# A decoder layer on one core: prologue, buffers and orders rebuilt

## The reference

```
q, k, v = x @ Wq + bq, x @ Wk + bk, x @ Wv + bv        # 16 heads of 8
q, k = rope(q), rope(k)                                # interleaved rotation
x = layernorm(x + softmax(q k^T / sqrt(8)) v)
x = layernorm(x + dense(cross_attention(x, ctx, mask)))  # ctx: 64 rows a batch, 16 heads
x = layernorm(x + relu(x @ W1 + b1) @ W2 + b2)         # 128 -> 512 -> 128
```

## Time and profile before

| what | us |
|---|---|
| median of three runs | 266.21 (264.18 to 266.30) |
| the profiled execution | 263.25 |
| its span, first to last instruction | 261.4 |
| mean granted TensorE clock, share of full | 0.944 |

### The profile page before, as it was taken

One profiled execution on the slowest core, in us unless ns is written; L12 is line 12 of the kernel. 1 busy time (PEld: TensorE's weight loads), 2 busy tenths in 40 slices (PEclk: granted clock), 3 DMA queues, 4 the chain that ended last, 5 costly groups with the idle time before them and its releaser, 6 DMA issues.

```text
span 261.4 us, 5399 instructions
## 1 busy us (share of the span) xinstructions
PE 220.7 (84%) x1734; PEld 169.8 (65%) x1734; DVE 189.4 (72%) x434; ACT 158.3 (61%) x296; POOL 82.9 (32%) x89
## 2 busy tenths in 40 slices
PE   0715757979998999999989999999999998988871
PEld 0503434847766768767757877967887776966661
DVE  5524845998995989979879977779557758474562
ACT  0089051847749666878914897648898455647330
POOL 9933026285543526013410121121011414113231
PEclk9985555999999999999999999999999999999998
DMA  5089991258476235143263034400031042300001
GB/s 191 0 240 292 338 225 38 73 160 265 127 216 192 94 110 168 49 144 119 73 188 115 4 93 159 128 3 16 5 93 61 3 140 78 80 4 21 20 20 43
DMA packets 21531, 28.67 MB, mean 110 GB/s; under 512 B 5248, under 2 KB 16768, under 8 KB 21376
## 3 DMA queue, kind: packets, MB, share of 16 engines
q1 hardware_dynamic: 21160, 27.87, 35.5%
q10 hardware_dynamic: 344, 0.46, 0.6%
HBM read 15.21 MB, written 11.27 MB: 101 GB/s over the span
## 4 chain that ended last, share of the span: by engine, by line
PE 50%; issue 14%; DVE 10%; DMA 9%; POOL 4%; ACT 2%; SPq 1%; DVEq 0%; POOLq 0%; ACTq 0%
PE bank L561 8%; PE scores L524 8%; PE scores L544 7%; PE bank L713 4%; DMA z_self<-qk_parts 4%; PE bank L702 3%; PE scores L619 3%; DMA q_rows<-z_self 3%; DVE neg_max L1413 2%; PE scores L622 2%; PE bank L656 2%; POOL rstd L1873 2%; PE scores L642 2%; PE scores L643 2%; DMA z_qx<-qx_parts 2%
## 5 line engine op out<-in xcount | busy, mean ns | idle before, releaser
L1413 DVE TENSOR_REDUCE neg_max<-scores 128x4 f32<-128x1024 f32 x64 | 76.3, 1219 | 15.6 <-PE scores L524 15.5
L1111 ACT ACTIVATE probs<-scores 128x1024 f32<-128x1024 f32 x64 | 64.0, 1026 | 7.5 <-PE scores L544 6.7
L524 PE MATMUL scores<-k_diag,q_rows 96*128 96x512 f32 x128 | 45.7, 463 | 11.4 <-DMA k_diag<-z_self 6.7
L544 PE MATMUL scores<-q_rows,k_diag 128*128 128x256 f32 x256 | 43.3, 300 | 1.3 <-ACT probs L1111 0.8
L544 PEld LDWEIGHTS scores<-q_rows,k_diag 128*128 128x128 f32 x256 | 35.6, 194 | 9.3 <-issue 7.6
L1873 POOL TENSOR_TENSOR rstd<-var_eps,minus_half 128x2 f32<-128x2 f32 x24 | 16.7, 698 | 66.6 <-DVE var_eps L1446 66.5
L524 PEld LDWEIGHTS scores<-k_diag,q_rows 96*128 96x128 f32 x128 | 22.9, 210 | 20.1 <-issue 18.0
L561 PE MATMUL bank<-probs,v_ones 128*32 128x256 f32 x512 | 30.9, 382 | 0.2
L1102 ACT CAST q_rows<-bank 8x128 fp32r<-8x128 f32 x64 | 16.3, 255 | 20.4 <-PE bank L532 19.3
L1413 DVE TENSOR_REDUCE neg_maxx<-scores 128x16 f32<-128x1024 f32 x16 | 19.4, 1223 | 8.7 <-PE scores L622 8.6
L561 PEld LDWEIGHTS bank<-probs,v_ones 128*32 128x32 f32 x512 | 16.3, 109 | 10.9 <-issue 3.4
(11 more groups left out here) (107 smaller groups left out, 385.1 us busy)
## 6 DMA issues: line engine op xcount, KB each, us to landing
z_self<-qk_parts SPq DMA_DIRECT2D x23, 256.0 KB, 3.2
q_rows<-z_self SPq DMA_DIRECT2D x8, 384.0 KB, 3.5
qx_slots<-z_qx SPq DMA_DIRECT2D x8, 384.0 KB, 3.4
k_diag<-z_self SPq DMA_DIRECT2D x30, 96.0 KB
z_qx<-qx_parts SPq DMA_DIRECT2D x8, 256.0 KB, 2.3
qk_swapped<-qk SPq DMA_DIRECT2D x14, 128.0 KB, 2.5
later_sb<-later SPq DMA_DIRECT2D x1, 1347.0 KB, 9.1
z_qx<-qx_parts SPq DMA_DIRECT2D x8, 128.0 KB, 2.5
```

Source lines behind the costliest of these rows:

```text
L524: mm = pe.matmul(score(use, b)[:, h * S:(h + 2) * S], qr_r[0:NROWS, b % 2, g, t * P:(t + 1) * P], kd_r[0:NROWS, b % 2, h:h + 2, g, :], sta ...
L544: mm = pe.matmul(score(use, b)[:, (2 * j + kt) * S:(2 * j + kt + 1) * S], kd_r[:, b % 2, 2 * half + j, g, kt * P:(kt + 1) * P], qr_r[:, b ...
L1111: ins = nc.scalar.activation(probs[:, g, 2 * half:2 * half + 2, :, :], score(use, b), ACT.Exp)
L1413: ins = nc.vector.tensor_reduce(out, score(use, b).rearrange("p (h k) -> p h k", k=SC if g == "x" else S), AX.X, ALU.max, negate=True)
```

## The change

- **Packs.** Instead of first, second and later there are six: wq and wk with their swapped columns, the tables at half the width (cos and sin once, not for q and k apart), wv with the identity, the cross-attention's constants, the FFN's. The factor 1/sqrt(8) leaves the tables and becomes the scale of the exp.
- **Queues.** ScalarE's queue loads the wv pack and xT of batch 0, the sync queue the rest. xT of batches 2 to 7 is issued before batch 0's images. The cross constants, context and FFN constants go later, one by one. x is loaded into xT's tile, so it waits for all projections.
- **Two batches rotated by VectorE.** Batches 0 and 1 both have swapped projections. VectorE does products, sums and low parts, q and k apart; ScalarE makes the high parts.
- **Projections.** q, k and v of the other batches stand between the first projections and batch 0's and 1's scores. They are copied to tiles of their own (qk for six batches, v_rows for eight). POOL instead of VectorE places v.
- **Warm-up.** Five matmuls on zeros stand first in TensorE's list. ScalarE's small exp moves near the end of its list.
- **Head rows.** ScalarE writes those of one buffer of k and of the cross k; a DMA copies them to the other.
- **Buffers.** x1_bias has eight, z_qx eight. Small PSUM uses may stand in any of the five spaces. The tables of uses and the step lists of all engines are new: cross-attention and FFN of early batches stand later in them than before.
- **Output.** It is stored in the order of partitions and reordered on the host; x is read in such an order too.

```diff
-FIRST = [("ident", P), ("wq", D), ("wk", D), ("bq", 1), ("bk", 1), ("wqs", D), ("wks", D), ("bqs", 1), ("bks", 1), ("head_of_row", HQ)]
-SECOND = [("cos", 2 * S), ("sin", 2 * S), ("wv", D), ("bv", D)]
+WQ = [("wq", D), ("wqs", D), ("bq", 1), ("bqs", 1)]
+WK = [("wk", D), ("wks", D), ("bk", 1), ("bks", 1)]
+ROPE = [("cos", S), ("sin", S)]
+WV = [("wv", D), ("bv", D), ("ident", P), ("head_of_row", HQ)]
+CROSS = [("wqx", D), ("wkx", D), ("wvx", D), ("bqx", 1), ("bkx", 1), ("bvx", D), ("mask", S), ("key_of_row", SC)]
+FFN = [("dense", D), ("w1", FF), ("w2", FC * D), ("b1", FC), ("dense_b", D), ("b2", D)]
...
         def misc(use, b):
-            return bank[:, SPACES.index(TURN[use, b][0]) - 3, :]
+            at = SPACES.index(TURN[use, b][0])
+            return scores[:, at, 0:512] if at < 3 else bank[:, at - 3, :]
...
+            def load_x():
+                for b in range(B):
+                    for use in ("qp", "kp", "v") if b < 2 else ("qkp", "v"):
+                        sp.wait_ge(*made(use, b))
+                sp.dma_start(x_res, x_d).then_inc(xres_in, 16)
...
+            load_xT(1)
+            load_wk()
+            load_rope()
+            load_wq()
+            load_other_xT()
+            first_image_high(0, 0)
+            first_image_low(0, 0)
+            first_image_low(0, 1)
+            load_q(0)
+            load_first_k()
+            first_image_high(1, 0)
+            first_image_high(1, 1)
+            first_image_low(1, 1)
+            first_image_low(1, 0)
+            swap(2)
+            load_q(1)
+            load_cross()
+            other_diag_heads()
+            load_ctxT()
+            load_k(1)
+            swap(3)
+            load_x()
+            images_low(2)
+            images_high(2)
+            load_ffn()
+            swap(4)
+            load_q(2)
+            load_k(2)
...
+            def warm_up():
+                pe.wait_ge(y_zeroed, 1)
+                for _ in range(5):
+                    pe.matmul(bank[:, 1, 0:S], y[:, 0, :], y[:].rearrange("p t d -> p (t d)"), start=True, stop=True)
+
+            def first_proj(b, j):
...
+                pe.matmul(o[:, 0:S], const(w), xT[:, b, :], start=True, stop=True)
+                mm = pe.matmul(o[:, S:2 * S], const(w + "s"), xT[:, b, :], start=True, stop=True)
...
+            warm_up()
+            first_proj(0, 1)
+            first_proj(0, 0)
+            first_proj(1, 1)
+            v_proj(1)
+            first_proj(1, 0)
+            qk_proj(2)
+            qk_proj(7)
+            v_proj(7)
+            qk_proj(5)
+            v_proj(5)
+            v_proj(2)
+            qk_proj(3)
+            v_proj(6)
             max_scores(0, 0, 0)
             max_scores(0, 0, 1)
+            v_proj(4)
+            max_scores(0, 1, 1)
+            max_scores(0, 1, 0)
+            qk_proj(4)
...
+            def first_high(b, j):
+                act.wait_ge(first_sum[j], b + 1)
...
+                nc.scalar.copy(qk_parts[:, 2 * j, :].bitcast(F32R), qk_rope[:, j, :]).then_inc(first_hi[j], 1)
...
+            def v_copy(b):
+                act.wait_ge(*made("v", b))
+                ins = nc.scalar.copy(v_rows[:, b, :], misc("v", b)[:, 0:S])
+                read_by(ins, "v", b)
...
-                ins = nc.scalar.activation(probs[:, g, 2 * half:2 * half + 2, :, :], score(use, b), ACT.Exp)
+                ins = nc.scalar.activation(probs[:, g, 2 * half:2 * half + 2, :, :], score(use, b), ACT.Exp, scale=KSCALE)
...
+            load_wv()
+            load_first_xT()
+            diag_heads()
+            first_high(0, 0)
+            first_high(0, 1)
+            first_image_high_k()
+            qk_copy(7)
+            v_copy(1)
+            qk_copy(2)
+            load_other_first_k()
+            v_copy(7)
+            v_copy(5)
+            first_high(1, 0)
+            v_copy(2)
+            first_high(1, 1)
+            v_copy(6)
...
+            def first_products(b, j):
...
+                nc.vector.scalar_tensor_tensor(qk_cos[:, j, :], misc(use, b)[:, 0:S], const(bias), const("cos"), ALU.add, ALU.mult
+                                               ).then_inc(first_terms[j], 1)
+                ins = nc.vector.scalar_tensor_tensor(qk_sin[:, j, :], misc(use, b)[:, S:2 * S], const(bias + "s"), const("sin"),
+                                                     ALU.add, ALU.mult)
...
+            clear_y()
+            clear_diag()
+            first_products(0, 1)
+            first_rotated(0, 1)
+            first_products(0, 0)
+            first_rotated(0, 0)
+            first_low(0, 0)
+            first_low(0, 1)
+            first_products(1, 1)
...
+            def place_v(b):
+                pool.wait_ge(*taken("v", b))
...
+                nc.gpsimd.tensor_tensor(
+                    v_ones[:, b % 2, :, :, CELL:CELL + HD], v_rows[:, b, :].rearrange("p (t h c) -> p t h c", t=QT, c=HD),
+                    const("bv").rearrange("p (o h c) -> p o h c", o=1, c=HD).to_broadcast([P, QT, H, HD]), ALU.add
+                    ).then_inc(v_placed, 1)
```

More of the change, by code:

```diff
@@ L170, in build @@
         x1 = sb("x1", [P, QT, D])
[L171 removed]
+        x1_bias = sb("x1_bias", [P, B, QT, D])
         x1T = sb("x1T", [P, S])
@@ L618, in maxx_scores @@
                 for half in range(2):
-                    pe.matmul(score(use, b)[:, half * 512:(half + 1) * 512], mask_r[:, t * P:(t + 1) * P], keys_r,
+                    pe.matmul(score(use, b)[:, half * 512:(half + 1) * 512], mask_r[:, t * P:(t + 1) * P], key_r.to_broadcast([P, 4, 2 * SC]),
                               start=True, stop=False, skip_group_check=True)
@@ L1205, in _ @@
+            v_copy(3)
+            maxT(0, 0)
+            v_copy(0)
+            exp(0, 0, 1)
+            maxT(0, 1)
+            exp(0, 0, 0)
+            maxT(0, 2)
+            exp(0, 1, 0)
+            maxT(0, 3)
+            exp(0, 2, 0)
+            exp(0, 1, 1)
+            qk_copy(6)
+            exp(0, 3, 0)
+            maxT(1, 1)
+            exp(0, 3, 1)
             exp(0, 2, 1)
-            maxT(1, 3)
-            exp(0, 1, 1)
-            qk_copy(4)
+            pv_copy(0, 0)
+            maxT(1, 0)
@@ new lines, in _ @@
+            qx_copy(1)
+            exp(3, 3, 0)
+            exp(3, 3, 1)
+            maxxT(0)
+            pv_copy(3, 0)
+            maxT(4, 0)
+            kx_heads()
+            x1T_copy(2)
+            pv_copy(3, 1)
+            expx(0, 0)
+            maxT(4, 1)
+            qx_copy(2)
+            exp(4, 0, 1)
+            maxT(4, 3)
+            expx(0, 1)
+            maxT(4, 2)
+            exp(4, 1, 1)
+            pvx_copy(0)
+            exp(4, 3, 1)
+            exp(4, 1, 0)
+            exp(4, 3, 0)
@@ new lines, in _ @@
+            exp(4, 0, 0)
+            exp(4, 2, 1)
+            exp(4, 2, 0)
+            pv_copy(4, 0)
+            maxT(5, 0)
+            att2T_copy(0)
+            exp(5, 0, 0)
+            pv_copy(4, 1)
+            x1T_copy(3)
+            maxT(5, 1)
+            maxT(5, 3)
+            exp(5, 0, 1)
+            qx_copy(3)
+            exp(5, 3, 1)
+            maxT(5, 2)
+            exp(5, 1, 0)
+            maxT(6, 1)
+            exp(5, 3, 0)
+            exp(5, 2, 1)
+            exp(5, 2, 0)
@@ new lines, in _ @@
+            maxT(6, 3)
+            maxT(6, 0)
+            exp(5, 1, 1)
+            pv_copy(5, 1)
+            maxxT(1)
+            pv_copy(5, 0)
+            exp(6, 1, 1)
+            expx(1, 0)
+            x1T_copy(4)
+            maxT(6, 2)
+            exp(6, 3, 0)
+            expx(1, 1)
+            exp(6, 0, 1)
+            x2T_copy(0)
+            exp(6, 0, 0)
+            qx_copy(4)
+            pvx_copy(1)
+            exp(6, 1, 0)
+            relu(0, 0)
+            exp(6, 2, 1)
@@ new lines, in _ @@
+            maxxT(2)
+            maxT(7, 0)
+            pv_copy(6, 0)
+            expx(2, 1)
+            exp(6, 3, 1)
+            exp(6, 2, 0)
+            relu(0, 1)
+            att2T_copy(1)
+            expx(2, 0)
+            maxT(7, 1)
+            pv_copy(6, 1)
+            exp(7, 1, 0)
+            x1T_copy(5)
+            exp(7, 0, 0)
+            maxT(7, 3)
+            maxxT(3)
+            qx_copy(5)
+            exp(7, 3, 1)
+            exp(7, 3, 0)
+            pvx_copy(2)
+            exp(7, 0, 1)
@@ new lines, in _ @@
+            expx(3, 1)
+            exp(7, 1, 1)
+            expx(3, 0)
+            maxxT(4)
+            x1T_copy(6)
+            pv_copy(7, 0)
+            maxT(7, 2)
+            att2T_copy(2)
+            x2T_copy(1)
+            pvx_copy(3)
+            exp(7, 2, 0)
+            exp(7, 2, 1)
+            qx_copy(6)
+            expx(4, 0)
+            pv_copy(7, 1)
+            expx(4, 1)
+            maxxT(5)
+            relu(1, 1)
+            relu(1, 0)
+            pvx_copy(4)
+            att2T_copy(3)
@@ new lines, in rope_sum, with qk_low @@
+            def rope_sum(b):
+                pool.wait_ge(rope_cos, b - 1)
```

(15 more changed lines are left out.)

1623 lines of the change are left out of this document (756 added, 867 removed), and 45 rows, old and new, of the table USES.

## The result

The changed kernel takes 248.22 us (247.64 to 249.25, four runs) against 265.54 for the kernel before beside it: ratio 0.9357 (95% interval 0.930 to 0.9415). Some executions of most kernels here come out slower by one or two per cent (one of the kernel before took 878.69 us); medians hold all executions, ratios leave those out, and so the two can differ.

> The changed kernel itself once more, as the reference for the runs beside it. Both theories: 247.5 to 249.5 us, batch 2's first max scores at 56 us, TensorE idle under 3 us between 100 and 224 us.

A forecast was written before the change was run, and what follows sets the result against it. TensorE was taken as the bound from 62.8 to 240 us, waiting for data before that. Profiled 263.25 - 8.8 (batch 2's start) - 4.5 (work done) + 1.0 (POOL contention) = 251.0 us, range 243 to 262.

The forecast's parts named there:

- Start: Before batch 0's scores: first product at about 6.3 us, last image at 11.7, first scores 1.4 us earlier, at 21.2.
- Batch 1: Batch 1's first max scores: x and FFN constants no longer ahead of its rows, so 32.5 us against 41.06.
- Batch 2: Batch 2's first max scores, behind x and FFN constants: 54 us (50 to 58) instead of 62.8, 8.8 us gained.
- Work done by then: TensorE by batch 2's start: all projections finished, 5.5 us, less one exp-score group and one context projection: 4.5 us net.
- Off VectorE, on to POOL: Eight v placements leave VectorE for POOL; contention with VectorE costs 1.0 us (zero to 6.0).
- rival (a): Middle, batches 3 to 6: VectorE can end last and eats part of the gain; 258 us (256 to 263), chance 0.19.
- The end: After batch 7's last exp scores: 17 us more cross-attention and FFN work, idle time stays; 0 within minus 4 and plus 4.
- (b): Start: dense TensorE work keeps the clock at 2.4 GHz, batch 2 at 50, PSUM freedom gives 2; 243 us, chance 0.08.
- (c): Whole kernel: later reduces and drain set the end, saved time turns into waits; within 1% of 266.2, chance 0.09.
- (d): Tail: postponed cross-attention and FFN chain on single buffers, 25 us more less 7 hidden; 269 us, chance 0.09.
- What would show it: Signs: scores near 21, 32.5, 50 to 58; clock 1.00 until about 17; TensorE busy near 215; final idle below 13 us.

The follow-up runs named there:

- constants_behind: Changed kernel with x and FFN constants issued behind batch 2's rows, cross constants, context and head-row copy behind batch 1's: 242.62 us, run again 243.31.
- v_on_dve: Changed kernel with all eight v placements on VectorE instead of POOL: 250.42 us, ratio 0.947 to the kernel before.
- bank experiments: Changed kernel with small PSUM uses put back in two small banks: 44 uses 299.31 us; only the 15 before batch 7's last exp scores 266.74 us.
- x_behind: Changed kernel with x and FFN constants issued behind batch 2's rows on the sync queue: 246.71 us, ratio 0.9314 to the kernel before.

## Why the prediction was right, and where its steps were off

251.0 was forecast, 243 to 262 as the range; 248.22 came. In the profiled executions the sum reads, step by step, 263.25 - 6.4 - 3.6 - 1.1 - 4.4 = 247.7:

| step | forecast | measured | from |
|---|---|---|---|
| batch 0's first scores | 21.2 | 19.67 | timeline |
| batch 1's | 32.5 | 33.42 | timeline |
| batch 2's | 54, -8.8 us | 56.33, -6.4 us | timeline |
| TensorE work left after it | -4.5 | -3.6 | 182.5 to 178.8 busy |
| middle, idle and contention | +1.0 | -1.1 | idle 5.0 to 3.9 |
| the tail | 0 (-4 to 4) | -4.4 | idle 11.2 to 6.8 |

(The idle time of the middle is the 16.2 and 10.7 us after batch 2's first scores less the tail's.)

That the sum came so near is in part luck. The start and the work done by then gave 3.3 us less than forecast, the middle and the tail 6.5 us more; either alone would have put the time off by more than the 3.2 us that are left.

*Start.* The first product came at 7.00 (forecast 6.3) and the last image at about 12.0 (11.7). From there to the scores it took less than before, so 19.67 was better than my 21.2. It is 2.9 us earlier than before, just outside the 0 to 2.7 that I had left.

*Batch 1* came 0.9 us after the forecast, with a k_diag wait of 3.27 us; that this wait is the constants' ahead of it, constants_behind shows by removing it.

*Batch 2* was 2.3 us later than my 54. Two things were mis-sized. I put x's issue at 37 us; it was 41.16, since batch 6's projections stood behind a later batch 1 and matmuls at half pace (clock 0.50 from 32 to 38 us), and the images behind it had to wait although they were ready. And I had not seen that VectorE's next high part waits for the same images: a tile whose sending DMA is late holds the engine that refills it. Both are parts of a transfer order that constants_behind repairs.

*Work done by then* was right in kind and 0.9 us too large.

*Off VectorE, on to POOL.* I had put the contention at 1.0. The one split seen beside a placement lost 0.5, and the splits' sum did not rise against the kernel before (15.2 after 15.6 us), so the term was small, but no run measures it. What I had not put in the sum was the gain on the other side, although rival (a) rests on it: VectorE binds up to 100 us, so relieving it of 4 us pays. v_on_dve puts the whole move at -2.4 us by the medians, up to -4.9 by the ratios.

*The end* is the term with the largest error, -4.4 for 0, just outside my 4. I had expected 17 us more work after the last exp scores and the old share of idle time or a little less; 11.7 came, at a better share. (My 11.8 us of old idle time counted 0.6 us behind the end of the span; it was 11.2.) The bank experiments show what the new orders lean on, small uses spread over five spaces: taken away as it was there, it costs 18 us ahead of the last exp scores and 30 behind them. I had priced that freedom at up to 4 us. They don't show that it made the tail better than the old one; order and freedom were not taken apart.

*Rivals.* (a), VectorE as the bound in the middle, is true as a mechanism up to 100 us (35.16 of 37.2 busy) and fits that x_behind passed on so little; it did not cost the 7 us that I gave it. (b)'s time, 243, was not reached by the change, but constants_behind reaches it, by the DMA order; what the clock around batch 1 adds there is open. (Its own two terms, 4 and 2 us off 251, give 245; the 243 had no working.) (c) and (d) are excluded by the result. (d)'s kind of loss can happen, as the bank runs show (267 and 299 us once small uses chain on two spaces), but they chain PSUM; the single buffers that (d) names were not tested.

*What would show it.* The clock until 17 us and idle after the last exp scores under 13 us (6.8) came as said. TensorE's busy total was 220, not 215: the warm-up adds 4.05 us of busy time that isn't work.

## What to carry to other kernels

- Where every engine runs a fixed list, the space that a small result takes in PSUM is part of the order: count how many small results are alive while big ones pass, before you price an order by its work alone.
- Order transfers by when their data is needed, not by what is handy: about a megabyte of constants and context ahead of batch 1's rows, on top of x and the FFN constants ahead of batch 2's, cost up to 5 us that no busy time showed. A load that must wait holds back ready ones behind it in its queue, and a tile that is sent late holds the engine that refills it.
- Before you buy clock or an earlier start, look which other engine is near its bound in the stretch behind it.

## What the runs showed that I had not expected

- The same kernel on two chips had clock 0.50 from 19 to 26 us once and 1.00 once, behind the same idle stretch, and its spans differed by 0.4 us. So a half-clock stretch in one trace is not a property of the kernel alone.
- A 128x8 cast on VectorE took 1078 ns once (median 172), from 24.95 us on, while POOL added 128x512 from 24.73 to 25.99. So not only the two-input subtract of the earlier trace rows is held up beside POOL; in the kernel before, too, one cast took 1193 ns. Which condition decides, no run here tells.
